# Two-layer conditioned transformer block on one core: three changes in the order of work (ScalarE's last exponentials, the stack's read, the second layer's value projection)

## The chip, the cores and the metric

One of the eight cores of a Trainium2 chip runs the whole kernel. The metric is the device time in microseconds (us) of one execution, a median over executions. The engines are TensorE (PE, with its weight loads as PEld), VectorE (DVE), ScalarE (ACT), GpSimd (POOL) and SyncE (SP), which here issues every DMA.

## The reference, cut to what matters

The input is 16 sequences of 256 tokens by 256 features, a condition of 64 numbers for each sequence, and one mask for all. Two layers follow each other, each added to its input.

```
# layer 0, for each sequence
n1 = g1(cond) * x * rsqrt(mean(x*x) + eps) + b1(cond)
a  = x + softmax(q(n1) k(n1)^T / 4) v(n1) @ Wo.T          # 16 heads of 16, no mask
n2 = g2(cond) * a * rsqrt(mean(a*a) + eps) + b2(cond)
x  = x + a + (silu(n2 @ gate.T) * (n2 @ hid.T)) @ out.T    # hidden 1024
# layer 1
o  = softmax(mask(q(x) k(x)^T / 4)) v(x) @ Wo.T            # the mask hides keys, the same for all queries
x  = x + (o * rsqrt(mean(o*o) + eps) * rms_scale) * (1 + sc(cond)) + shift(cond)
```

## The kernel before, in words

Matmuls of fp32 precision are made from three passes over high and low parts (`mm3`, lines 526 to 528). All 16 sequences stay in SBUF (`X`). The work is a software pipeline over 32 items: item n below 16 is sequence n in layer 0, the others are layer 1. Step s (from -3 to 33) works on several items at once (`stages`, line 79): A, the query and key projection of item s+2; V and B1, the value projection and the first score pass (for the row maxima) of item s+1; B2, the second score pass with the exponentials of item s; C, the division, output projection and mean squares of item s-1; C2 and C3, the gated feed-forward part of layer-0 items s-2 and s-3; R, the output norm of layer 1, item s-2; N, the input norm of item s+3. Each step has eight slots g = 0 to 7; slot g carries heads 2g and 2g+1 of both score passes. Every engine's order is written out by hand in its own `step` function, and engines meet at semaphores only. Steps 3 to 12 and 19 to 28 are loops of two steps.

TensorE's results of A, V, C and the norms go through two PSUM banks in turn, `work0` and `work1`. `bank_uses` (line 105) lists the uses of a step in order; the uses take the two banks alternately, and a use waits (`open_bank`) until the use before it on its bank is freed. From step 19 on the shift rows' and output norm's small uses have a third bank (`acc`). In steps 19 to 29 the list is Q, T1a, T1b, K, T2, Wo, V, ms on banks 0, 1, 0, 1, 0, 1, 0, 1. K is freed by VectorE's `rest` (line 924), T2 by its `ol` (line 910), which the output projection also needs as an operand.

Queries and keys: each projection is split in three bf16 parts (ScalarE L1100 and L1149, VectorE L920 and L924, GpSimd L1239), written to DRAM (`write_parts`, L414), and when both writes have landed read back (`read_stack`, L424) so that the parts of 96 contraction rows stand on 96 partitions. One half (8 heads) is three DMAs of 384, 256 and 128 KB in pieces of 4096 bytes, all on SP's queue. SP's order in a step is: shift rows of half 1, query write, key write, stack read of half 0, shift rows of half 0 (`rows_in(0)`, L470), result store (R), stack read of half 1. TensorE waits for half 0 ahead of the first score pass of slot 0 in the next step and for half 1 at slot 4 (`scores_for_max`, L569 or L584). Ahead of the second score pass (`scores`, L607) of slots 0 and 4 it waits for the shift rows, the negated row maxima that SP copies into the stack.

The mask of the input hides all keys of the first half, which the kernel finds at run time; layer 1's score passes then take the second key half alone (`full` is False).

ScalarE in slot 7 of a step with a layer-0 item in C: it waits for VectorE's product of the residual and the second norm's root (`crm`, L955), applies gain and bias (`affine`, L1087, twice), copies to the high part `xch` (L1134), and then does the two exponentials of slot 7 (`exps`, L1058). GpSimd makes the low part `xcl` (L1322) from `xch`; the first feed-forward matmul of the next step needs it. The second half's probability-value product (`values(st, 1)`, L623) stands at slot 0 of the next step and needs all exponentials.

Slot 3 of a layer-1 step on TensorE: first and second score pass, output projection of item s-1, value projection of item s+1. ScalarE then copies the output projection to `y` (L1162) and the values to `vaug` (L1166); GpSimd squares `y` (L1298) for the mean squares at slot 6 (L710).

Of the kernel before, what the change touches and what calls it, by code (L numbers as in the profile page):

```python
# [46 lines left out]
T = 256  # L47
D = 256
H = 16
# [21 lines left out]
FIRST, LAST = -3, 2 * B + 1  # L71
SPARE = B + 3


# [30 lines left out]
def bank_uses(L):  # L105

    uses = []
    for g in range(SLOTS):
# [8 lines left out]
        if g == 2 and L["C"] is not None:  # L117
            uses.append("T2")
        if g == 3 and L["C"] is not None:
            uses.append("Wo")  # L120
        if g == q_slot(L, 1):
            uses.append("K")
        if g == 1 and L["R"] is not None:
            uses.append("bcR")
        if g == 3 and L["V"] is not None:
            uses.append("V")
# [105 lines left out]
def build(nc, xT, w0, w_ffn, w_out, w1, condT, cond_w, cond_b, rms_scale, mask, maskT, yT):  # L232
    ctx = ExitStack()
    with ctx:
# [114 lines left out]
        q_written, k_written = sem("q_written"), sem("k_written")  # L349
        stack_loaded = [sem(f"stack_loaded{i}") for i in range(2)]  # L350
        s1_full, s1_free = sem("s1_full"), sem("s1_free")
# [33 lines left out]
        def _(sp):  # L385
# [29 lines left out]

            def read_stack(par, half_):

                row = 0
                for parts in (3, 2, 1):
                    k = DH * parts  # L420
                    src = bass.AP(scr[par].tensor, half_ * 6 * DH * 8 * T,
                                  [[8 * T, k], [(6 * DH - k) * 8 * T, 2], [1, 8 * T]])
                    dst = stack[par][row:row + k, :, 8 * half_:8 * half_ + 8, :]
                    sp.dma_start(dst.rearrange("r o h t -> r o (h t)"), src).then_inc(stack_loaded[half_], 16)  # L424
                    row += k
# [13 lines left out]
            def step(st):  # L439
# [50 lines left out]
                if L["A"] is not None:  # L490
                    for half_ in range(2):
                        after(sp, stack_loaded[half_], scratch_read)
                    after(sp, q_low, a_split)
                    write_parts(par, 0, qp, q_written)
                    after(sp, k_low, a_split)
                    write_parts(par, 3 * DH, kp, k_written)
                    after(sp, q_written, a_written)
                    after(sp, k_written, a_written)
                    if L["B2"] is not None:
                        after(sp, s2_full, heads_used[0])  # L500
                    mask_row_in(st, 0)
                    read_stack(par, 0)
                load_swap(6)
                if L["B1"] is not None:
# [3 lines left out]
                if L["A"] is not None:  # L508
                    if L["B2"] is not None:
                        after(sp, s2_full, heads_used[1])  # L510
                    mask_row_in(st, 1)
                    read_stack(par, 1)
                for r in registers:
# [7 lines left out]
        def _(pe):  # L521
# [31 lines left out]
            def scores_for_max(st, g):  # L553
                n, par = st.n(1), 1 - st.par
                if g in (0, 4):
                    after(pe, stack_loaded[g // 4], 48 * (n + 1))
                    if st.s0 in (BRANCH, BRANCH + 1):
                        pe.wait_ge(mask_row_loaded[g // 4], 16 * (st.s0 - BRANCH + 1))
# [184 lines left out]
            def step(st):  # L743
# [14 lines left out]
                for g in range(SLOTS):  # L758
# [24 lines left out]
                    if g == 5 and L["B1"] is not None and st.s0 >= SPARE:  # L783
                        shift_transpose(st, 0)
                    if g == 3 and L["C"] is not None:
                        if st.s0 - 1 == B:
# [6 lines left out]
                    if g == 1 and L["R"] is not None:  # L793
                        broadcast_rstd(st, "bcR", 2)
                    if g == 3 and L["V"] is not None:
                        if st.s0 + 1 == B:
# [235 lines left out]
        def _(act):  # L1032
# [51 lines left out]
            def affine(st, buf, gain, shift, b, done, count):  # L1084
# [5 lines left out]
                after(act, done, count)  # L1090

            def shift_store(st, half_):
                bank, free = opened(st, f"sh{half_}")
# [13 lines left out]
            def step(st):  # L1107
# [5 lines left out]
                for g in range(SLOTS):  # L1113
# [12 lines left out]
                    if g == 6 and st.s0 >= SPARE:  # L1126
                        if L["B1"] is not None:
                            shift_store(st, 0)
                    if g == 7 and L["C"] == 0:
                        n = st.n(-1)  # L1130
# [3 lines left out]
                        a.copy(xch[1 - st.par][:, :, :], crm[:, :, :]).then_inc(c_hi, 1)  # L1134
                    if L["B2"] is not None:
                        exps(st, g)
                        if g == 1:
                            shift_store(st, 1)
                    if g == 5 and st.s0 < SPARE:
# [10 lines left out]
                    if g == 2 and L["R"] is not None:  # L1150
                        n = st.n(-2)
                        b, k = st.bank("bcR")
                        after(act, work_free[b], k + 1)
                        affine(st, crm, C_SCALE, C_SHIFT, n - B, c_affine, 2 * (n + 1))
                    if g == 3 and L["C"] == 1:
                        bank, free = opened(st, "Wo")
# [5 lines left out]
                        a.copy(flat(y[:, :, :]), bank[:, :]).then_inc(free, 1)  # L1162
                    if g == 3 and L["V"] is not None:
                        bank, free = opened(st, "V")
                        after(act, pv_done, 2 * st.n(0))
                        a.copy(vaug[1 - st.par][:, :, :, 0:DH],  # L1166
                               bank[:, :].rearrange("p (t h d) -> p t h d", t=TC, h=H)).then_inc(free, 1)
                    if g == 4 and L["N"] == 1:
# [218 lines left out]
```

## Time and profile before

| | |
|---|---|
| time, median of 3 executions | 999.9 us (996.64, 999.9, 1002.29) |
| the profiled execution: time, span | 992.56 us, 990.5 us |
| busy PE, PEld, DVE, ACT, POOL | 92%, 79%, 58%, 53%, 42% |
| mean granted TensorE clock | 0.963 |
| DMA, share of 16 engines | 40.4% |

The span is that of the trace; the execution's own time has 2.06 us more around it. Matmuls are pipelined and their ends are modelled, so a busy PE row says that TensorE has work and not that it runs at its peak; the waits ahead of single instructions say more. In rows of the timeline the bracket gives the idle time of that engine ahead of the row and what ended it. The clock of 1.00 is 2.4 GHz, 0.50 is 1.2 GHz.

### The profile page before, as it was taken

To read this page: it belongs to the slowest core of one execution; us is meant where nothing else is said; L and a number is where in the kernel's file an instruction comes from. 1 tells how busy PE (TensorE), PEld (TensorE's weight loads), DVE (VectorE), ACT (ScalarE), POOL (GpSimd) and SP (SyncE) were. 2 spreads that over 40 slices of the span, in tenths; PEclk is the share of its full clock that TensorE was granted. 3 is DMA by queue.
4 is the path that set the end of the run, shared out by engine and by line. 5 is a ranking of instruction groups with operands and counts; after the bars stand their busy time and mean duration, and the time that the engine had idled before them with its cause. 6 is when DMAs were issued, how large, how long until landed. Compare 5 with 4: busy or idle time off the path is not lost.

```text
span 990.5 us, 24274 instructions
## 1 busy us (share of the span) xinstructions
PE 910.0 (92%) x8188; PEld 777.7 (79%) x8188; DVE 575.3 (58%) x1136; ACT 529.9 (53%) x1098; POOL 416.2 (42%) x633
## 2 busy tenths in 40 slices
PE   3578899999999999999999999999998999999884
PEld 3456598898988988889888898898887777777653
DVE  3366557556665565555755656645646666666541
ACT  2246446546455464555654654554546566666552
POOL 5233343434443434434443443444444545454422
PEclk9779799999999999999999999999999999999986
DMA  6555422422233223322242233234236767676801
GB/s 201 117 107 125 91 66 61 92 66 44 69 86 59 65 59 71 82 44 65 63 86 64 51 91 86 50 67 91 67 64 143 174 146 171 150 171 150 175 21 34
DMA packets 81724, 91.27 MB, mean 92 GB/s; under 512 B 6432, under 2 KB 68672, under 8 KB 81664
## 3 DMA queue, kind: packets, MB, share of 16 engines
q1 hardware_dynamic: 81664, 90.49, 40.4%
q8 instruction: 35, 0.57, 0.3%
q14 instruction: 25, 0.20, 0.1%
HBM read 60.30 MB, written 29.36 MB: 91 GB/s over the span
## 4 chain that ended last, share of the span: by engine, by line
PE 72%; DMA 8%; DVE 6%; issue 5%; ACT 5%; POOL 2%; SPq 1%; ACTq 0%; POOLq 0%; DVEq 0%
PE work L526 12%; PE work L527 11%; PE work L528 11%; PE pvps L623 8%; PE s2ps L607 6%; PE s1ps L584 5%; DMA stack<-scr 5%; PE work L710 3%; PE work L656 3%; PE acc L526 3%; PE acc L527 2%; PE acc L528 2%; DMA scr<-kp 2%; PE s1ps L569 2%; ACT E L1058 1%
## 5 line engine op out<-in xcount | busy, mean ns | idle before, releaser
L1058 ACT ACTIVATE E<-s2ps 128x512 f32<-128x512 f32 x384 | 214.0, 596 | 179.9 <-PE s2ps L607 113.6
L883 DVE TENSOR_REDUCE nmax<-s1ps 128x2 f32<-128x512 f32 x256 | 164.0, 683 | 32.2 <-PE s1ps L584 32.0
L963 DVE SCALAR_TENSOR_TENSOR th<-th,work 128x256 f32<-128x256 f32 x128 | 54.0, 422 | 174.5 <-ACT th L1076 174.5
L526 PE MATMUL work<-xch,Gh 128*128 128x256 f32 x512 | 154.6, 302 | 0.0
L1336 POOL TENSOR_TENSOR hl<-hf,hh 128x256 fp32r<-128x256 f32 x128 | 94.9, 742 | 132.9 <-PE acc L528 76.7
L527 PE MATMUL work<-xcl,Gh 128*128 128x256 f32 x512 | 146.3, 286 | 0.0
L528 PE MATMUL work<-xch,Gl 128*128 128x256 f32 x512 | 146.2, 286 | 0.0
L607 PE MATMUL s2ps<-stack 100*128 100x256 bf16 x768 | 129.2, 277 | 0.2
L876 DVE TENSOR_REDUCE nmax<-s1ps 128x4 f32<-128x512 f32 x128 | 85.6, 686 | 38.0 <-PE s1ps L569 37.8
L623 PE MATMUL pvps<-E,vaug 128*32 128x256 f32 x1536 | 99.1, 392 | 8.0 <-ACT E L1058 7.0
L526 PEld LDWEIGHTS work<-xch,Gh 128*128 128x128 f32 x512 | 98.8, 193 | 8.1 <-issue 6.6
L527 PEld LDWEIGHTS work<-xcl,Gh 128*128 128x128 f32 x512 | 99.2, 194 | 0.3
L528 PEld LDWEIGHTS work<-xch,Gl 128*128 128x128 f32 x512 | 99.2, 194 | 0.0
L584 PE MATMUL s1ps<-stack 96*128 96x256 bf16 x512 | 83.4, 283 | 11.6 <-DVE nmax L883 5.4
L1239 POOL TENSOR_TENSOR qp<-rest,qp 128x512 bf16<-128x512 f32 x32 | 37.2, 1164 | 134.5 <-ACT qp L1105 118.5
L1076 ACT ACTIVATE th<-work 128x256 f32<-128x256 f32 x128 | 49.2, 384 | 70.2 <-PE work L528 70.2
L526 PE MATMUL work<-xnh,Wh 128*128 128x256 f32 x256 | 78.9, 308 | 3.6 <-DVE on L903 0.9
L1239 POOL TENSOR_TENSOR kp<-rest,kp 128x512 bf16<-128x512 f32 x32 | 37.2, 1164 | 103.4 <-DVE rest L924 48.8
L623 PEld LDWEIGHTS pvps<-E,vaug 128*32 128x32 f32 x1536 | 44.5, 111 | 43.9 <-issue 15.5
L607 PEld LDWEIGHTS s2ps<-stack 100*128 100x128 bf16 x768 | 67.9, 99 | 12.0 <-issue 0.8
L527 PE MATMUL work<-xnl,Wh 128*128 128x256 f32 x256 | 74.1, 289 | 0.0
L528 PE MATMUL work<-xnh,Wl 128*128 128x256 f32 x256 | 73.9, 289 | 0.0
(133 smaller groups left out, 2171.8 us busy)
## 6 DMA issues: line engine op xcount, KB each, us to landing
stack<-scr SPq DMA_DIRECT2D x64, 384.0 KB, 4.6
stack<-scr SPq DMA_DIRECT2D x64, 256.0 KB, 5.3
scr<-qp SPq DMA_DIRECT2D x64, 192.0 KB, 2.3
scr<-kp SPq DMA_DIRECT2D x64, 192.0 KB, 2.3
stack<-scr SPq DMA_DIRECT2D x64, 128.0 KB, 5.6
X<-xT SPq DMA_DIRECT2D x16, 256.0 KB, 4.6
yT<-crm SPq DMA_DIRECT2D x16, 256.0 KB, 2.5
E<-w_ffn SPq DMA_DIRECT2D x2, 1024.0 KB, 6.0
```

Source lines behind the costliest of these rows:

```text
L526: mm(out, lh, rh, start=first, stop=False, skip_group_check=True)
L527: mm(out, lh, rl, start=False, stop=False, skip_group_check=True)
L528: return mm(out, ll, rh, start=False, stop=last, skip_group_check=True)
L584: last = mm(bank[:, T * i:T * (i + 1)], qst[par][0:PARTS, h, P * qh:P * (qh + 1)], kst[par][0:PARTS, h, :], start=st.L["B1"] == 0, stop=Tr ...
L607: last = mm(bank[:, T * i:T * (i + 1)], kst[par][0:ROWS, h, P * kh:P * (kh + 1)], qst[par][0:ROWS, h, :], start=not add_mask, stop=True, s ...
L623: last = mm(pvps[32 * i:32 * (i + 1), T * (j % 2):T * (j % 2 + 1)], v_of[:, kh, h, :], E[:, exp_slot(layer, st.full, h // 2, kh), T * (h % ...
L876: v.tensor_reduce(nmax[:, g // 4, :, 2 * (g % 4):2 * (g % 4) + 2], s1ps[g % 2][:, :].rearrange("p (q h t) -> p q h t", q=2, h=2), AX_X, AL ...
L883: v.tensor_reduce(nmax[:, g // 4, qh, 2 * (g % 4):2 * (g % 4) + 2], s1ps[u % 2][:, :].rearrange("p (h t) -> p h t", h=2), AX_X, ALU.max, n ...
L963: v.scalar_tensor_tensor(th[:, i % 2, :], th[:, i % 2, :], 1.0, bank[:, 0:T], ALU.add, ALU.mult).then_inc(silu_ready, 1)
L1058: a.activation(E[:, exp_slot(st.L["B2"], st.full, g, kh), :], s2ps[g % 2 if short else u % 2][:, :], ACT.Exp, scale=SCORE_SCALE).then_inc( ...
L1239: p.tensor_tensor(parts[:, lo_at, :, :], rest[:, :, :], parts[:, 1, :, :], ALU.subtract).then_inc(low, 1)
L1336: p.tensor_tensor(hl[:, i % 2, :], hf[:, i % 2, :], hh[:, i % 2, :].bitcast(F32), ALU.subtract).then_inc(h_low, 1)
```

## The change

It has three parts. On ScalarE, the exponentials of a slot are put ahead of the layer-0 output norm's gain and bias (this differs in slot 7 alone). On SP, the stack's half 0 is read in two pieces, heads 0 to 3 and heads 4 to 7, each of three DMAs in pieces of 2048 bytes, both behind the same waits; TensorE waits for the first piece at slot 0, for the second at slot 2, and for half 1 at slot 4 as it did. In steps 17 to 30, where C is in layer 1, the value projection precedes the output projection on TensorE, in the list of banks and on ScalarE.

```diff
+HEADS = ((0, 0, 4), (0, 4, 4), (1, 0, 8))
 # bank_uses
+        if g == 3 and L["V"] is not None and L["C"] == 1:
+            uses.append("V")
         if g == 3 and L["C"] is not None:
             uses.append("Wo")
...
-        if g == 3 and L["V"] is not None:
+        if g == 3 and L["V"] is not None and L["C"] != 1:
             uses.append("V")
 # SP
-            def read_stack(par, half_):
+            def read_stack(par, piece):
+                half_, first, heads = HEADS[piece]
                 row = 0
                 for parts in (3, 2, 1):
                     k = DH * parts
-                    src = bass.AP(scr[par].tensor, half_ * 6 * DH * 8 * T,
-                                  [[8 * T, k], [(6 * DH - k) * 8 * T, 2], [1, 8 * T]])
-                    dst = stack[par][row:row + k, :, 8 * half_:8 * half_ + 8, :]
-                    sp.dma_start(...).then_inc(stack_loaded[half_], 16)
+                    src = bass.AP(scr[par].tensor, half_ * 6 * DH * 8 * T + first * T,
+                                  [[8 * T, k], [(6 * DH - k) * 8 * T, 2], [1, heads * T]])
+                    h0 = 8 * half_ + first
+                    dst = stack[par][row:row + k, :, h0:h0 + heads, :]
+                    sp.dma_start(...).then_inc(stack_loaded[piece], 16)
                     row += k
...
                     read_stack(par, 0)
+                    read_stack(par, 1)
                 load_swap(6)
                 if L["B1"] is not None:
                     rows_in(0)
...
-                    read_stack(par, 1)
+                    read_stack(par, 2)
 # TensorE
             def scores_for_max(st, g):
+                if g in (0, 2, 4):
+                    after(pe, stack_loaded[g // 2], 48 * (n + 1))
                 if g in (0, 4):
-                    after(pe, stack_loaded[g // 4], 48 * (n + 1))
...
+                    if g == 3 and L["V"] is not None and L["C"] == 1:
+                        value_projection(st)
                     if g == 3 and L["C"] is not None:
...
                         output_projection(st)
...
-                    if g == 3 and L["V"] is not None:
+                    if g == 3 and L["V"] is not None and L["C"] != 1:
 # ScalarE
+                    if L["B2"] is not None:
+                        exps(st, g)
+                        if g == 1:
+                            shift_store(st, 1)
                     if g == 7 and L["C"] == 0:
                         ...
                         affine(st, crm, C_G2, C_B2, n, c_affine, 2 * (n + 1))
                         a.copy(xch[1 - st.par][:, :, :], crm[:, :, :]).then_inc(c_hi, 1)
-                    if L["B2"] is not None:
-                        exps(st, g)
-                        if g == 1:
-                            shift_store(st, 1)
...
+                    if g == 3 and L["V"] is not None and L["C"] == 1:
+                        value_store(st)      # the copy to vaug
                     if g == 3 and L["C"] == 1:
                         ...
                         a.copy(flat(y[:, :, :]), bank[:, :]).then_inc(free, 1)
```

With the new list, steps 19 to 29 use the banks as Q 0, T1a 1, T1b 0, K 1, T2 0, V 1, Wo 0, ms 1.

## Rows read from the trace of the kernel before

**Rows 1.** The page: busy us, share of the span, instructions.
```profile
PE 910.0 (92%) x8188; PEld 777.7 (79%) x8188; DVE 575.3 (58%) x1136; ACT 529.9 (53%) x1098; POOL 416.2 (42%) x633
```

**Rows 2.** Stretches: us from:to, length, busy (x count) by engine, PEclk, DMA, GB/s.
```profile
436.41:475.94 39.53, 39.07 (x357) 34.92 (x357) 23.90 (x47) 21.88 (x49) 16.64 (x25) 1.00 0.31 67
395.36:436.41 41.05, 40.59 (x357) 36.43 (x357) 23.87 (x47) 21.99 (x49) 16.61 (x25) 0.96 0.30 64
425.30:428.60 3.30, 3.30 (x18) 3.30 (x17) 0.84 (x3) 2.21 (x6) 1.49 (x2) 0.50 0.01 2
850.00:882.90 32.90, 30.55 (x312) 24.77 (x316) 21.93 (x45) 20.92 (x41) 17.03 (x29) 1.00 0.70 161
```

**Rows 3.** Timeline, TensorE, values at slot 0: start, us, what, idle before.
```profile
155.09 0.42 PE L623 MATMUL pvps<-E,vaug 128*32 128x256 f32 x4 [0.28 <-ACT E L1058]
...
273.75 0.63 PE L623 MATMUL pvps<-E,vaug 128*32 128x256 f32 x7 [0.36 <-ACT E L1058]
...
554.92 0.64 PE L623 MATMUL pvps<-E,vaug 128*32 128x256 f32 x8 [0.28 <-ACT E L1058]
...
114.07 1.51 PE L623 MATMUL pvps<-E,vaug 128*32 128x256 f32 x12 [1.03 <-issue]
```

**Rows 4.** Timeline, ScalarE, slot 7 of the step ending at 273.7.
```profile
270.88 1.10 ACT L1087 ACTIVATE crm<-crm,cond 128x256 f32<-128x256 f32 x2 [1.40 <-DVE crm L955]
...
272.54 1.08 ACT L1058 ACTIVATE E<-s2ps 128x512 f32<-128x512 f32 x2
```

**Rows 5.** Timeline, weight loads: last scores of that slot, next feed-forward matmul.
```profile
270.09 0.43 PEld L607 LDWEIGHTS s2ps<-stack 100*128 100x128 bf16 x4
...
276.39 0.19 PEld L526 LDWEIGHTS work<-xch,Gh 128*128 128x128 f32 x1
```

**Rows 6.** Timeline, GpSimd, same place.
```profile
272.71 1.28 POOL L1322 TENSOR_TENSOR xcl<-crm,xch 128x512 fp32r<-128x512 f32 x1 [2.43 <-ACT xch L1134]
```

**Rows 7.** Timeline, TensorE, one layer-1 step.
```profile
839.89 0.40 PE L569 MATMUL s1ps<-stack 97*128 97x128 bf16 x4 [0.29 <-DMA stack<-scr]
840.12 0.38 PE L607 MATMUL s2ps<-stack 100*128 100x256 bf16 x2
...
843.57 0.60 PE L718 MATMUL acc<-dg,ones 128*128 128x256 f32 x2
...
846.40 0.39 PE L526 MATMUL work<-oh,Wh 128*128 128x256 f32 x1 [0.91 <-DVE ol L910]
...
851.67 1.05 PE L710 MATMUL work<-mean,dg 128*128 128x1 f32 x8
```

**Rows 8.** Timeline, VectorE, same step.
```profile
845.07 0.68 DVE L924 TENSOR_TENSOR rest<-work,kp 128x512 f32<-128x512 f32 x1
845.66 0.68 DVE L910 TENSOR_TENSOR ol<-work,oh 128x512 fp32r<-128x512 f32 x1
```

**Rows 9.** Timeline, ScalarE and GpSimd, same step.
```profile
848.91 0.58 ACT L1162 COPY y<-work 128x512 f32<-128x512 f32 x1
...
849.65 1.04 POOL L1298 TENSOR_TENSOR dg<-y 128x512 f32<-128x512 f32 x1
```

**Rows 10.** Timeline, SP, DMA issues of one layer-1 step.
```profile
833.31 1.27 SPq L424 DMA_DIRECT2D stack<-scr  x3
836.06 0.74 SPq L470 DMA_DIRECT2D stack<-rows  x1
```

**Rows 11.** Chain of waits: start, us to landing, what.
```profile
834.15 5.62 DMA stack<-scr
...
83.36 4.67 DMA stack<-rows
```

**Rows 12.** The page, DMA issues: KB each, median us to landing.
```profile
scr<-kp SPq DMA_DIRECT2D x64, 192.0 KB, 2.3
```

**Rows 13.** Waits, whole span: us in total, times, longest.
```profile
PE s1ps L569 <- DMA stack<-scr: 4.4, 7, 1.4
```

**Rows 14.** Timeline, TensorE, first score pass of the run.
```profile
44.62 1.04 PE L584 MATMUL s1ps<-stack 96*128 96x256 bf16 x4 [4.62 <-DMA stack<-scr]
```

More of the change, by code:

```diff
@@ L349, in build @@
         q_written, k_written = sem("q_written"), sem("k_written")
-        stack_loaded = [sem(f"stack_loaded{i}") for i in range(2)]
+        stack_loaded = [sem(f"stack_loaded{i}") for i in range(3)]
         s1_full, s1_free = sem("s1_full"), sem("s1_free")
@@ L420, in read_stack @@
                     k = DH * parts
-                    src = bass.AP(scr[par].tensor, half_ * 6 * DH * 8 * T,
-                                  [[8 * T, k], [(6 * DH - k) * 8 * T, 2], [1, 8 * T]])
-                    dst = stack[par][row:row + k, :, 8 * half_:8 * half_ + 8, :]
-                    sp.dma_start(dst.rearrange("r o h t -> r o (h t)"), src).then_inc(stack_loaded[half_], 16)
+                    src = bass.AP(scr[par].tensor, half_ * 6 * DH * 8 * T + first * T,
+                                  [[8 * T, k], [(6 * DH - k) * 8 * T, 2], [1, heads * T]])
+                    h0 = 8 * half_ + first
+                    dst = stack[par][row:row + k, :, h0:h0 + heads, :]
+                    sp.dma_start(dst.rearrange("r o h t -> r o (h t)"), src).then_inc(stack_loaded[piece], 16)
                     row += k
@@ L490, in step @@
                 if L["A"] is not None:
-                    for half_ in range(2):
-                        after(sp, stack_loaded[half_], scratch_read)
+                    for piece in range(3):
+                        after(sp, stack_loaded[piece], scratch_read)
                     after(sp, q_low, a_split)
@@ L1090, in affine, with value_store @@
                 after(act, done, count)
+            def value_store(st):
+                bank, free = opened(st, "V")
+                after(act, pv_done, 2 * st.n(0))
+                a.copy(vaug[1 - st.par][:, :, :, 0:DH],
+                       bank[:, :].rearrange("p (t h d) -> p t h d", t=TC, h=H)).then_inc(free, 1)
             def shift_store(st, half_):
@@ L1162, in step @@
                         a.copy(flat(y[:, :, :]), bank[:, :]).then_inc(free, 1)
[L1163 to L1167, printed above, removed]
+                    if g == 3 and L["V"] is not None and L["C"] != 1:
+                        value_store(st)
                     if g == 4 and L["N"] == 1:
```

## The prediction

> **What bounds the kernel now.** I read the page first, then the stretches, then the waits ahead of single TensorE instructions. TensorE is busy for 92% of the span [rows 1]. A layer-0 step takes 39.53 us with 39.07 busy, so there only TensorE's own gaps can be won [rows 2]. A layer-1 pair of steps takes 32.90 us, 16.45 a step, with 30.55 busy and DMA at 0.70 [rows 2]: there TensorE and a loop through DRAM are nearly level. Three waits are what the change can touch: the values at slot 0 wait for ScalarE's exponentials [rows 3], the output projection waits 0.91 us for `ol`, and the first score pass waits for the stack [rows 7, 13].
>
> **Part 1, exponentials first.** In slot 7 ScalarE runs the two gains from 270.88, then `xch`, and the exponentials only from 272.54 to 273.62 [rows 4]; TensorE starts the values at 273.75 after 0.36 us of idling for them [rows 3]. Their scores were loaded from 270.09 to 270.52 [rows 5], with the last product some 0.3 us later, so the exponentials could run from about 270.8 to 271.9, long before TensorE wants them. The whole wait goes. It stands ahead of eleven boundaries from 155.09 to 554.92, nine at about 0.36 us and the two ends at 0.28 [rows 3]. As the rows' ends are modelled and a restart costs a little more than the idle figure, I count 0.40 each, 4.4 us; the bounds are 0 and 0.5 each (5.5). The boundary at 114.07, at half clock, waits 1.03 us, and there the exponentials would come some 1.1 us sooner; I take 0.9 (0 to 1.0). What is late in return is `xch`, by the 1.08 us of the exponentials, and with it `xcl`: 272.71 + 1.28 = 273.99 becomes 275.1 [rows 4, 6]. The next step's first feed-forward matmul, loaded at 276.39 [rows 5] and now 0.4 earlier, still finds it 0.9 us old. GpSimd's queue behind `xcl` moves back by the same 1.1 us, and nothing in it is waited for sooner than that matmul. ScalarE's total is the same. Part 1: -5.3 us.
>
> **Part 2, the value projection first.** The first read says 0.91 us won in each of eleven steps (19 to 29). It isn't so: the value projection takes the bank that K held, which VectorE's `rest` frees at 845.07 + 0.68 = 845.75, while `ol` ends at 845.66 + 0.68 = 846.34 [rows 8]. TensorE can start 0.59 us sooner and no more. The output projection behind it then finds `ol` done. ScalarE now copies the values (0.58 us, taken from the like copy) before `y`, so `y` ends at 848.91 + 0.58 + 0.58 = 850.07, its square (now 849.65 to 850.69) at about 851.2, and the mean squares, at 851.67 now [rows 7, 9], would be wanted at 851.08: a new wait of 0.1 us. So TensorE's own path of a step shrinks by about 0.5 us. Whether that counts depends on the loop in part 3. In steps 17 and 18 the banks leave the start of slot 3 where it was, and step 30 has no K: nothing there.
>
> **Part 3, the stack in two pieces.** The key write lands, three reads go out from 833.31, the last lands at 834.15 + 5.62 = 839.77 [rows 10, 11], the first score pass starts at 839.89 and the second at 840.12; K's projection is done when the next instruction starts at 843.57 [rows 7], and the loop starts again. A 192 KB write lands in 2.3 us [rows 12], which I take as a DMA's fixed part. From the first issue to the last landing are 6.46 us, 4.2 of them for 768 KB; a first piece of half the bytes lands 2.1 us sooner, at 837.7 (bounds: not sooner at all, or half of 6.46, 3.2 us). The three added issues cost SP 1.27 us [rows 10], from 834.58 to 835.9, and the shift rows' issue was at 836.06: it just fits. The second piece is wanted at slot 2, near 844, and lands near 840: hidden.
>
> But the first score pass was not alone. Right behind it the second pass needs the shift rows, issued at 836.06 behind all six stack DMAs on one queue [rows 10]. They landed before 840.12, and no sooner than 2.3 us after issue, 838.4. The row at 83.36 shows such rows taking 4.67 us with a read ahead of them [rows 11]; I put them with the end of the read, about 839.6. The change moves neither the read's last byte nor these rows. TensorE would do the first score pass early and then stand at the second until 839.6 or a little later, where it now starts at 840.12. So the step loses 0.5 us at best, and the 0.5 us of part 2 falls into the same wait. Over the steps 20 to 30 the trace puts 4.4 us of idling to the stack, in seven waits [rows 13]; I take 4.4 less 1.4 for 2048-byte pieces and more issues ahead of the shift rows: -3.0 us. Bounds: +4 (rows 0.4 us later in eleven steps) and -10.9 (4.4 and 0.59 times eleven, if the rows don't bind).
>
> At the start of the run TensorE stands 4.62 us for the first stack [rows 14], and no shift rows are needed in that step; the 2.1 us are won there, but a half-clock stretch follows, so I take 1.5 (0 to 3.2). In layer 0's later steps no first score pass waits for a stack, so an earlier one wins nothing.
>
> The Trainium skill (DMA: Bandwidth & Descriptors, the anatomy of one DMA) fits a GpSimd-issued DMA as 2.0 us plus bytes at 436 GB/s. By it, 384 KB less would land only 0.9 us sooner, and the run's start would win 0.9 at most; the sum would be 9.2 instead of 9.8. This trace's 4.2 us for 768 KB is 187 KB/us, less than half of that rate, so I go by the trace.
>
> **The sum.** 5.3 + 3.0 + 1.5 = 9.8 us, the profiled execution's 992.56 would become 982.8 (span 990.5 to 980.7). The median shown is 999.9, 7.3 above that execution. Three layer-0 steps in a row took 41.05 instead of 39.53 us, each with 3.3 us at a clock of 0.50 (1.2 GHz) around the mean squares [rows 2]; if the median's excess is the same thing, it has nearly five more. The steps keep the same work but get another length, and a run of equal steps would break up; I allow two fewer, 3 us. Predicted: 999.9 - 9.8 - 3 = 987.1, say 987 us.
>
> **Rivals.**
> (a) The shift rows don't bind and TensorE's path decides: layer 1 gives 10.9 - 1.1 = 9.8 instead of 3.0, and with fewer half-clock stretches 978 to 981 us. For it: no wait of the second score pass for rows is in the layer-1 rows. Against: the first pass hid it. Chance 0.25.
> (b) The read in two pieces and the new order bring nothing, and part 1 brings its 4 to 5 us alone: 995 us. For it: the DMA share of 0.70 and the shift rows' place in the queue. Chance 0.2. If even part 1's wait is replaced (`xcl` more than 0.9 us later than I think), the change does nothing: 999 to 1000, included here.
> (c) Slower: a read is paid by the piece and not by the byte. Half 0 has twice the pieces, so its 4.2 us become 8.4, and the shift rows behind it land 4.2 us later; each of eleven steps waits 4.2 - 0.5 longer, +41, less 6.8 from parts 1 and the start: near 1034. It makes the kernel slower from about 1.1 us a step on ((6.8 + 5)/11). Against: a 192 KB write in pieces of 512 bytes, eight times as many per byte, lands in 2.3 us [rows 12]. Chance 0.05.
> The forecast itself (984 to 993) has 0.5.
>
> **How the numbers follow.** 0.5% of 999.9 is 5 us, about what a measurement can tell; faster is below 994.9. The forecast's case and (a) are faster nearly whole (0.5 and 0.25, less 0.04), (b) in a quarter: 0.76. Within 0.5%: 0.18. Slower: (c) and a bad draw of half-clock stretches, 0.06. The range takes (a) in to 975 and (b) to 997.
>
> **What would show it.** Right: values at slot 0 with no idle for ScalarE in the eleven boundaries and `xch` a microsecond later; layer-0 steps of 39.1 us; in layer 1 the value projection starting as `rest` ends; first score passes starting early, and the second ones idling behind them for the shift rows; a step of 16.0 to 16.3 us. Wrong: second score passes right behind the first ones and steps of 15.6 (then (a)); shift rows landing more than 4 us after issue (then (b) or (c)); feed-forward matmuls waiting for `xcl`; layer-0 steps that stay at 39.5.

## The result, and the profile after

The changed kernel takes 975.87 us (median of four runs, 973.7 to 977.97) against 1000.53 us for the kernel before (four runs, 996.64 to 1002.29). The ratio is 0.9758 [0.9722, 0.9795]: 24.7 us less. The forecast was 987 us, a gain of 13. The profiled execution took 973.7 us with a span of 971.6 us, at a mean granted clock of 0.971; before it was 992.56, 990.5 and 0.963. Line numbers are higher after the change: `rest` is L933, `ol` L919, the score passes L576 or L591 and L614, `mm3` L532 to L534, the exponentials L1067.

The page, busy time, as in [rows 1]; then the shares of the chain that ended last. TensorE's share of the chain was 72% before and DMA's 8%.

```profile
PE 905.2 (93%) x8188; PEld 774.5 (80%) x8188; DVE 574.7 (59%) x1136; ACT 526.0 (54%) x1098; POOL 413.2 (43%) x633
```

```profile
PE 85%; DVE 5%; ACT 3%; issue 3%; DMA 2%; POOL 1%; SPq 1%; POOLq 0%; DVEq 0%; ACTq 0%
```

The stretches, as [rows 2]: a layer-0 step with a half-clock stretch, one without, the half-clock stretch itself, and two layer-1 steps.

```profile
345.85:386.46 40.61, 40.51 (x357) 36.32 (x357) 23.98 (x47) 21.89 (x50) 16.54 (x24) 0.96 0.29 65
425.55:464.64 39.09, 38.99 (x357) 34.88 (x357) 23.89 (x47) 21.78 (x50) 16.57 (x24) 1.00 0.30 68
376.10:379.50 3.40, 3.40 (x18) 3.31 (x17) 1.24 (x3) 2.13 (x6) 1.63 (x2) 0.50 0.01 4
836.06:868.15 32.09, 30.78 (x310) 24.72 (x309) 21.92 (x45) 20.43 (x42) 16.62 (x28) 1.00 0.66 165
```

Layer-0 steps went from 39.53 to 39.09 us, and from 41.05 to 40.61 where a half-clock stretch falls in. Two layer-1 steps went from 32.90 to 32.09 us.

The boundaries of [rows 3] on TensorE: the values at slot 0 follow with no idle time in the bracket.

```profile
266.13 1.93 PE L630 MATMUL pvps<-E,vaug 128*32 128x256 f32 x32
...
542.84 0.42 PE L630 MATMUL pvps<-E,vaug 128*32 128x256 f32 x4
```

ScalarE there, as [rows 4], then GpSimd, as [rows 6]. The exponentials now run before the two gains. Against the values at 266.13 the gains start 1.73 us earlier, where they started 2.87 earlier before, so against the values `xch` is 1.1 us later. `xcl` ends at 267.51 and the next step's first feed-forward matmul is at 268.80: 1.3 us of room, where the prediction had 0.9. It had delayed the gains by the whole 1.08 us of the exponentials on the step's own clock; as the values come 0.43 us sooner too, they are only 0.7 later there.

```profile
263.43 1.09 ACT L1067 ACTIVATE E<-s2ps 128x512 f32<-128x512 f32 x2 [1.14 <-PE s2ps L614]
264.40 1.09 ACT L1096 ACTIVATE crm<-crm,cond 128x256 f32<-128x256 f32 x2
265.52 0.62 ACT L1153 CAST xch<-crm 128x512 fp32r<-128x512 f32 x1
```

```profile
266.22 1.29 POOL L1336 TENSOR_TENSOR xcl<-crm,xch 128x512 fp32r<-128x512 f32 x1 [3.12 <-ACT xch L1153]
```

One layer-1 step on TensorE, as [rows 7]: the third line is the transposes of item s-1's output in slot 1, the last is now the value projection, which waits for `rest`. The two passes of slot 0, shown ahead of them, have no idle in front.

```profile
842.29 0.40 PE L576 MATMUL s1ps<-stack 97*128 97x128 bf16 x4
842.52 0.38 PE L614 MATMUL s2ps<-stack 100*128 100x256 bf16 x2
843.06 0.66 PE L663 MATMUL work<-ident,oT 128*128 128x128 f32 x4 [0.15 <-ACT oT L1077]
...
848.59 0.35 PE L532 MATMUL work<-Wh,xnh 128*128 128x256 f32 x1 [0.40 <-DVE rest L933]
```

VectorE there, as [rows 8]: `rest` ends at 848.44, and the value projection starts at 848.59, 0.45 us before `ol` ends.

```profile
847.76 0.68 DVE L933 TENSOR_TENSOR rest<-work,kp 128x512 f32<-128x512 f32 x1
848.36 0.68 DVE L919 TENSOR_TENSOR ol<-work,oh 128x512 fp32r<-128x512 f32 x1
```

SP's issues in such a step, as [rows 10]:

```profile
836.48 2.68 SPq L429 DMA_DIRECT2D stack<-scr  x6
839.25 0.74 SPq L475 DMA_DIRECT2D stack<-rows  x1
```

The first score pass of the run, as [rows 14]: 42.22 instead of 44.62 us, 2.15 of idling instead of 4.62.

```profile
42.22 1.03 PE L591 MATMUL s1ps<-stack 96*128 96x256 bf16 x4 [2.15 <-DMA stack<-scr]
```

Where 18.9 us of span went, read from the starts of the values in both timelines: 2.1 by the first one (77.60 to 75.47). 4.2 between there and 155.09 (now 148.78). A stretch at half clock, 107.7 to 118.0 us before, is absent after, so these 4.2 have two causes. The kernel with the exponentials undone (`e_noexps` below) has no such stretch either, and from the values at 82.24 to those at 149.44 it takes 67.20 us, against 65.46 after and 69.65 before: 1.7 are the exponentials' and 2.5 the clock's. 5.8 over the next ten boundaries, 0.43 each and 1.5 for one half-clock stretch fewer. Minus 1.3 for a half-clock stretch at 734.5 us that is new. 5.1 over the layer-1 steps up to 932. 4.6 in step 30, of which 0.8 are its path (14.41 against 15.25 us in kernels without a half-clock stretch there) and 3.7 the half-clock stretch of before at 937.2. Minus 1.3 near the end, another stretch at half clock, and minus 0.2 behind the last values. Together the edits make about 14 and the clock about 5. The boundary behind the missing stretch, as the last of [rows 3], in the changed kernel and then in `e_noexps`:

```profile
109.64 1.24 PE L630 MATMUL pvps<-E,vaug 128*32 128x256 f32 x17 [0.57 <-issue]
```

```profile
110.28 1.07 PE L630 MATMUL pvps<-E,vaug 128*32 128x256 f32 x16 [2.27 <-issue]
```

The rows of the two stretches before, and of the first one's place after (columns as in [rows 2], clock third from last):

```profile
107.70:118.00 10.30, 8.56 (x51) 4.43 (x50) 4.19 (x8) 6.10 (x13) 3.68 (x7) 0.50 0.49 93
937.20:947.40 10.20, 8.25 (x52) 5.72 (x41) 3.23 (x7) 2.97 (x6) 0.66 (x3) 0.50 0.49 106
```

```profile
107.70:118.00 10.30, 8.82 (x86) 6.43 (x84) 6.81 (x15) 7.07 (x14) 3.35 (x6) 1.00 0.51 102
```

### The profile page after: what moved, and what is told of

The parts are those of the page before. It is cut to its first block, busy times and chain, and to the rows that moved or that the text cites. A ratio compares the mean times of both kernels' runs of the same rounds, so it can differ in the third digit from the quotient of the medians.

```text
span 971.6 us, 24412 instructions
## 1 busy us (share of the span) xinstructions
PE 905.2 (93%) x8188; PEld 774.5 (80%) x8188; DVE 574.7 (59%) x1136; ACT 526.0 (54%) x1098; POOL 413.2 (43%) x633
## 4 chain that ended last, share of the span: by engine, by line
PE 85%; DVE 5%; ACT 3%; issue 3%; DMA 2%; POOL 1%; SPq 1%; POOLq 0%; DVEq 0%; ACTq 0%
PE work L532 14%; PE work L533 12%; PE work L534 12%; PE pvps L630 9%; PE s2ps L614 7%; PE s1ps L591 6%; PE work L717 4%; PE work L663 3%; PE acc L532 3%; PE acc L533 3%; PE acc L534 3%; PE s1ps L576 2%; PE work L725 1%; PE work L677 1%; DVE rest L933 1%
## 5 line engine op out<-in xcount | busy, mean ns | idle before, releaser
L1067 ACT ACTIVATE E<-s2ps 128x512 f32<-128x512 f32 x384 | 214.9, 598 | 192.9 <-PE s2ps L614 126.8
L532 PE MATMUL work<-xch,Gh 128*128 128x256 f32 x512 | 154.0, 301 | 0.1
L534 PE MATMUL work<-xch,Gl 128*128 128x256 f32 x512 | 145.6, 284 | 0.0
L614 PE MATMUL s2ps<-stack 100*128 100x256 bf16 x768 | 127.6, 275 | 1.0 <-DMA stack<-rows 0.8
L532 PEld LDWEIGHTS work<-xch,Gh 128*128 128x128 f32 x512 | 98.2, 192 | 8.5 <-issue 6.9
L534 PEld LDWEIGHTS work<-xch,Gl 128*128 128x128 f32 x512 | 98.6, 193 | 0.0
L591 PE MATMUL s1ps<-stack 96*128 96x256 bf16 x512 | 83.2, 282 | 8.4 <-DVE nmax L892 5.4
L532 PE MATMUL work<-xnh,Wh 128*128 128x256 f32 x256 | 79.3, 310 | 3.6 <-DVE on L912 0.9
L614 PEld LDWEIGHTS s2ps<-stack 100*128 100x128 bf16 x768 | 67.1, 98 | 13.1 <-issue 1.7
L534 PE MATMUL work<-xnh,Wl 128*128 128x256 f32 x256 | 74.0, 289 | 0.0
```

The costliest lines, as they stand in the source:

```text
L532: mm(out, lh, rh, start=first, stop=False, skip_group_check=True)
L534: return mm(out, ll, rh, start=False, stop=last, skip_group_check=True)
L591: last = mm(bank[:, T * i:T * (i + 1)], qst[par][0:PARTS, h, P * qh:P * (qh + 1)], kst[par][0:PARTS, h, :], start=st.L["B1"] == 0, stop=Tr ...
L614: last = mm(bank[:, T * i:T * (i + 1)], kst[par][0:ROWS, h, P * kh:P * (kh + 1)], qst[par][0:ROWS, h, :], start=not add_mask, stop=True, s ...
L1067: a.activation(E[:, exp_slot(st.L["B2"], st.full, g, kh), :], s2ps[g % 2 if short else u % 2][:, :], ACT.Exp, scale=SCORE_SCALE).then_inc( ...
```

## Experiments

All were timed beside runs of the kernel before on the same chip. A ratio is to that kernel. "Layer-1 step" is the mean of eight steps, from the values of one step near 771 to 790 us to the same eight steps on: 16.59 us before and 16.11 after, each with a few tenths of disturbance in single steps; the undisturbed steps are 16.41 and 16.47 in turn before, and 16.01 and 16.08 after.

**One part at a time.** The first kernel is the changed one with the other two parts undone:

```diff
 # e_exps: changed kernel, value projection and stack read as before
-                    if g == 3 and L["V"] is not None and L["C"] == 1:
-                        value_projection(st)
...
-HEADS = ((0, 0, 4), (0, 4, 4), (1, 0, 8))
+HEADS = ((0, 0, 8), (1, 0, 8))
```

> Only the exponentials of slot 7 go ahead of the layer-0 output norm's gains; the stack's read and the order of the two projections are those of before. Theory (each part pays where its own wait stands): the eleven boundaries from 155 to 555 us lose 0.43 us each, 4.7 us, the boundary at 114 about 1, so 5 to 6 us, ratio 0.994 to 0.995; layer-1 steps stay at 16.46 us. Rival (most of the 24.7 us comes from half-clock stretches that go away once these waits are gone): 10 us or more, ratio 0.990 or lower, with the stretches at 107 to 118 and at 937 to 947 us missing in the trace.

Measured: 987.85 us, ratio 0.9912 [0.9882, 0.9943]. Layer-0 steps 39.10 us, layer-1 steps 16.59 as before. The order of the exponentials is worth its 0.43 us at each boundary, and there is no half-clock stretch at 107 us either, while the one of 10.2 us near 937 is one of 3.4 at 945. The theory's path of 5 to 6 us is there (4.3 at ten boundaries, 1.7 ahead of them), but its ratio of 0.994 to 0.995 is touched by the interval's edge only. The 0.9912 lies between it and the rival's 0.990: beyond the path, fewer and shorter half-clock stretches brought the rest.

```diff
 # e_value: kernel before, with in layer 1
+                    if g == 3 and L["V"] is not None and L["C"] == 1:
+                        value_projection(st)
                     if g == 3 and L["C"] is not None:
```

> Only the value projection goes ahead of the output projection in layer 1. Theory (in layer 1 the loop through DRAM binds, so TensorE's shorter path falls into the wait for the stack): a layer-1 step stays within 0.1 us of 16.46, ratio 0.998 to 1.001, with the first score pass idling 0.5 us longer for the stack. Rival (TensorE's own path binds): 0.5 us a step in eleven steps, ratio 0.994.

Measured: 995.11 us, ratio 0.998 [0.9957, 1.0004], layer-1 step 16.46. That is what the theory said, but partly by chance: one of the eight steps took 18.04 us, with 2.36 of waiting for the stack. The other seven are 16.05 to 16.46, 16.23 in the mean, 0.2 us less than the undisturbed steps before.

```diff
 # e_split: kernel before, with
+HEADS = ((0, 0, 4), (0, 4, 4), (1, 0, 8))
```

> Only the stack's half 0 is read in two pieces. Theory (the six DMAs of 2048-byte pieces land as a whole about 0.8 us sooner than the three of 4096, and the shift rows behind them too; TensorE's path with its 0.98 us stand ahead of the output projection then binds): layer-1 steps of 16.2 to 16.3 us instead of 16.46, 2.1 us won at the start, 4 to 5 us in all without clock effects, ratio 0.994 to 0.996. Rival (the early first piece is what pays, in full): steps of 15.9 to 16.0.

Measured: 992.18 us, ratio 0.9937 [0.9906, 0.9969]. The start is 2.1 us shorter; layer-1 step 16.44, undisturbed ones 16.41 and 16.47 as before. Both the theory's steps (16.2 to 16.3) and the rival's (15.9 to 16.0) are missed, though the ratio is the theory's: what was won lies at the start and in the clock and the disturbed steps.

```diff
 # e_late: e_split, with
-                if g in (0, 2, 4):
-                    after(pe, stack_loaded[g // 2], 48 * (n + 1))
+                if g == 0:
+                    after(pe, stack_loaded[0], 48 * (n + 1))
+                    after(pe, stack_loaded[1], 48 * (n + 1))
```

> As the kernel with only the read in two pieces, but TensorE waits for both pieces at slot 0. Theory (faster landing of the whole half): layer-1 steps as in the kernel with the early wait, within 0.1 us, the half complete 5.5 to 5.7 us after the key write instead of 6.3 to 6.8; the start of the run wins about 1 us less. Rival (the early wait is what pays): steps of 16.4 us or more, time as before, ratio 0.998 to 1.002.

Measured: 993.32 us, ratio 0.9962 [0.9936, 0.9987]. Layer-1 steps as in e_split apart from one disturbed step, start 0.6 us shorter than before instead of 2.1. As layer 1 had won nothing in e_split, this run tells only of the start. The three parts alone sum to 0.9% + 0.2% + 0.6% = 1.7%; together they bring 2.4%. With intervals of 0.2 to 0.4 points each way and half-clock stretches that differ, these sums say little by themselves; the steps say more. What is missing sits for the most part in layer 1, and TensorE's waits over the eight steps say why (us in total, times, longest). Before:

```profile
PE work L526 <- DVE ol L910: 7.2, 8, 0.9
PE s1ps L569 <- DMA stack<-scr: 3.2, 5, 1.4
```

The value projection first, alone:

```profile
PE s1ps L575 <- DMA stack<-scr: 6.5, 8, 2.4
PE work L531 <- DVE rest L932: 3.2, 8, 0.4
```

The stack in two pieces, alone:

```profile
PE work L530 <- DVE ol L915: 7.2, 8, 0.9
PE work L661 <- ACT oT L1073: 1.1, 7, 0.2
```

Both, in the changed kernel:

```profile
PE work L532 <- DVE rest L933: 3.2, 8, 0.4
PE work L663 <- ACT oT L1077: 0.9, 6, 0.2
PE s2ps L614 <- DMA stack<-rows: 0.8, 1, 0.8
```

Alone, the new order turns 7.2 us of waiting for `ol` into 3.2 for `rest` and gives 3.3 of the 4.0 to the stack, which is now waited for in every step. Alone, the read in pieces ends the wait for the stack, but the transposes of slot 1 then wait for ScalarE's copy `oT`, and `ol` costs what it did. Only together both are gone, and what is left is `rest`, 0.4 us a step.

**The changed kernel without one part.** The exponentials undone:

```diff
 # e_noexps: changed kernel, with exps(st, g) behind the affine of slot 7 again
```

> The changed kernel with the exponentials of slot 7 put back behind the output norm's scale; the early value projection and the read in two pieces stay. Theory J (these two belong together, and the exponentials have their own part): layer-1 steps stay at 16.05 us; layer-0 boundaries come back to a step of 39.53 us, 0.43 us each over eleven of them and some 2 us at the one at 110 us, so the span is 971.6 + 4.7 + 2.2 = 978.5 us if the half-clock stretches stay as in the changed kernel (ratio about 0.983). Theory S (the 39.53 us step brings the half-clock stretches back, eight of 1.5 us in a row as in the kernels with one of the other parts alone, against two): 9 us more, span 987 to 988, ratio 0.989 to 0.992. Rival: the layer-1 gain needs the exponentials too: steps of 16.4 us, 5 us more on either.

Measured: 985.76 us, ratio 0.989 [0.9856, 0.9924]. Layer-1 steps are 16.01 to 16.10 but for one with a wait for shift rows, so layer 1 doesn't need the exponentials. Its layer-0 steps are 39.51 us and six of them in a row have a half-clock stretch, against two in the changed kernel; the rows (columns as in [rows 2]) show one step without and one with:

```profile
268.05:307.56 39.51, 39.05 (x356) 34.90 (x357) 23.88 (x47) 21.86 (x49) 16.61 (x25) 1.00 0.30 67
371.50:412.50 41.00, 40.55 (x358) 36.41 (x357) 23.92 (x48) 21.98 (x48) 16.61 (x25) 0.96 0.30 64
```

So theory S is right in direction, with six stretches for its eight; its ratio (from 0.989) is just reached, but the profiled span of 980.5 us is nearer theory J's 978.5. The part is worth 1.3% here and 0.9% alone, of which 6.0 us, 0.6%, are TensorE's waits (0.43 at each of ten boundaries and 1.7 ahead of them), the rest the clock.

```diff
 # e_nov: changed kernel, with the value projection behind the output projection again
```

> The changed kernel without the early value projection: exponentials first and the read in two pieces alone. Theory J (the two pieces shorten a layer-1 step only together with the early value projection, since without it the output projection waits for `ol` whatever the stack does): layer-1 steps 16.4 us, some 5 us slower than the changed kernel, ratio to the kernel before 0.980 to 0.985. Rival (the value projection is not needed for it): steps 16.05 to 16.1, ratio 0.975 to 0.978.

Measured: 981.95 us, ratio 0.9875 [0.9815, 0.9935], layer-1 step 16.43 with the 7.2 us of waiting for `ol`. The step confirms theory J. The ratio's interval is wide, but it lies wholly above the rival's 0.975 to 0.978.

**Why the shift rows came sooner.** The forecast's loop needed the shift rows to land when they did before. In the changed kernel six DMAs carry the bytes of three. Is it their number or their packets? The next kernel has the same six issues on SP, the same bytes and the same waits as e_late, but splits queries from keys and leaves the packets at 4096 bytes:

```diff
 # e_six: kernel before, half 0 read by
+                    for o in range(2):       # 0: queries, 1: keys
+                        src = bass.AP(scr[par].tensor, o * (6 * DH - k) * 8 * T, [[8 * T, k], [1, 8 * T]])
+                        dst = stack[par][row:row + k, o, 0:8, :]
```

> The kernel before with one edit: half 0 of a stack is read by six DMAs instead of three, one for the queries and one for the keys of each block of rows, each packet still 4096 bytes; the first pass waits for all six. It tells why the split half lands sooner as a whole than the unsplit one. Theory N (the number of transfers in flight): the half and the shift rows behind it land some 0.8 us sooner after the key write, as with the half in two pieces that are both waited for, the start is some 0.6 us shorter, ratio to the kernel before 0.994 to 0.998, layer-1 steps 16.4. Theory P (the 2048-byte packets): the half lands as late as in the kernel before, three more issues, ratio 0.999 to 1.003, start unmoved.

Measured: 994.66 us, ratio 0.9978 [0.9953, 1.0003], layer-1 steps 16.41 to 16.63 but for one. The first values come 1.1 us later than before, but the first score pass of the run only 0.2 (44.85 against 44.62): the first half-clock stretch is 17.1 us long here instead of 13.7, so theory P's unmoved start holds as far as the read goes. Theory P's time and theory N's don't exclude each other by the ratio, but the landings do. Issues of the page, KB each and median us to landing, e_six first, then the changed kernel (the row of 128 KB is left out, as it mixes the second reads of half 0 with the third of half 1):

```profile
stack<-scr SPq DMA_DIRECT2D x64, 192.0 KB, 3.6
...
stack<-scr SPq DMA_DIRECT2D x64, 64.0 KB, 4.1
```

```profile
stack<-scr SPq DMA_DIRECT2D x64, 192.0 KB, 3.1
...
stack<-scr SPq DMA_DIRECT2D x64, 64.0 KB, 3.3
```

Same sizes, same number, and the ones with packets of 2048 bytes land 0.5 and 0.8 us sooner. The two kernels also differ in what a DMA holds, four heads of queries and keys against eight of either; that was not tried apart, and neither were three DMAs of 2048-byte packets. In one step of the timeline: the three reads of before,

```profile
stack<-scr SPq DMA_DIRECT2D x1, 384.0 KB, 4.6
stack<-scr SPq DMA_DIRECT2D x1, 256.0 KB, 5.3
stack<-scr SPq DMA_DIRECT2D x1, 128.0 KB, 5.6
```

against the second piece's three after:

```profile
stack<-scr SPq DMA_DIRECT2D x1, 192.0 KB, 3.4
stack<-scr SPq DMA_DIRECT2D x1, 128.0 KB, 3.3
stack<-scr SPq DMA_DIRECT2D x1, 64.0 KB, 3.3
```

Before, the last read lands 6.46 us after the first issue (833.31 to 839.77 [rows 10, 11]). After, the sixth issue leaves at about 838.7 (836.48 and five sixths of 2.68) and lands 3.3 us on, at 842.0, 5.5 us after the first. It is 0.9 us sooner although its last issue is 1.4 us later. Over the layer-1 steps between 766 and 905 us, by the landing times of their traces, half 0 is complete 6.2 to 6.8 us after its first issue before (median 6.3), 6.2 to 6.8 in e_six (6.4) and 5.4 to 6.1 in the changed kernel (5.6).

```diff
 # e_four: changed kernel, with
-HEADS = ((0, 0, 4), (0, 4, 4), (1, 0, 8))
+HEADS = ((0, 0, 2), (0, 2, 2), (0, 4, 4), (1, 0, 8))
```

> The changed kernel with the first piece of half 0 split again into heads 0 and 1 and heads 2 and 3, waited for at slots 0 and 1. Theory W (layer 1 waits no longer for the stack; only the start does): the start shortens by 0 to 0.8 us, the rest is unmoved, ratio to the kernel before 0.974 to 0.977. Rival P (1024-byte packets cost more per byte, and the rows behind them land later): layer-1 steps of 16.3 us or more and 4 us slower, ratio above 0.979.

Measured: 980.09 us, ratio 0.9834 [0.9797, 0.987], layer-1 step 16.28 with one of 17.19; the other seven are 16.15 in the mean, 0.1 above the changed kernel's. Rival P's time, and TensorE's waits over eight steps name the place:

```profile
PE s2ps L615 <- DMA stack<-rows: 4.1, 8, 1.4
PE work L533 <- DVE rest L934: 3.2, 8, 0.4
```

SP's issues in one of these steps, then the second pass of slot 0 in it:

```profile
837.75 4.11 SPq L429 DMA_DIRECT2D stack<-scr  x9
```

```profile
844.44 0.39 PE L615 MATMUL s2ps<-stack 100*128 100x256 bf16 x2 [0.48 <-DMA stack<-rows]
```

Nine issues take 4.1 us of SP, and the shift rows behind them come too late in every step: this is what the forecast had feared of six. Packet size and number of issues both change here, but the trace points to the issues: the last read leaves 1.4 us later than in the changed kernel (3.65 us after the first issue against 2.23) and takes no longer to land (about 3.0 us against 3.3), so the half is complete only after 6.4 to 6.7 us. The second pass starts within 0.2 us of that moment in every step, so the shift rows do land with the end of the read, as the forecast assumed. Of three, six and nine DMAs, six were best.

```diff
 # e_after_late: changed kernel, both pieces waited for at slot 0 (as e_late)
```

> The changed kernel, its half 0 still read in two pieces, but both waited for ahead of slot 0's first pass. In the changed kernel the second piece landed at 842.0 us and that pass began at 842.29. Theory P (what layer 1 gains from the read is that smaller packets bring the whole half and the shift rows behind it sooner, not that the first pass needs half of it): layer-1 steps 16.0 to 16.15 us as in the changed kernel, and only the start is longer, by 1 to 2 us; ratio to the kernel before 0.976 to 0.981. Rival F (the first pass must start on the first piece): steps of 16.3 us or more, 4 us and the start on top, ratio 0.981 to 0.986.

Measured: 978.51 us, ratio 0.9806 [0.977, 0.9842]. The start is 2.1 us longer; seven of the eight layer-1 steps are 16.01 to 16.09, and the eighth has a wait of 2.0 us for the stack and a half-clock stretch. The ratio lies where the two forecasts meet; the steps decide. So layer 1 doesn't need the first piece early; it needs the whole half sooner, and the early first wait pays at the start.

**Two tries for more.** Half 1 in two pieces as well:

```diff
 # e_half1: changed kernel, with
+HEADS = ((0, 0, 4), (0, 4, 4), (1, 0, 4), (1, 4, 4))
```

> The changed kernel with half 1 of a stack also read in two pieces of four heads, waited for at slots 4 and 6. Theory W (nothing waits for half 1 in the changed kernel, what counts is what its first passes wait for): the same time, 974 to 978 us, ratio to the kernel before 0.974 to 0.978. Rival L (the half and the mask and shift rows behind it land sooner and layer 1 or the start has a wait on them): 2 to 4 us less, ratio 0.971 to 0.974. Rival I (three more issues on SyncE push the next step's rows back): 2 us or more slower, ratio above 0.979.

Measured: 973.4 us, ratio 0.9774 [0.9737, 0.9812]. The intervals of this and of the changed kernel cover each other: the same, theory W. Its layer-1 steps are the changed kernel's.

Then the wait for `rest`, filled with the two passes of slot 4:

```diff
 # e_move: changed kernel; e_best: with half 1 in two pieces too
                         scores(st, g)
+                    if g == 4 and L["V"] is not None and L["C"] == 1:
+                        value_projection(st)
+                    if g == wo_slot(L) and g == 4:      # layer 1
+                        output_projection(st)
```

> The changed kernel with layer 1's value and output projections moved from the end of slot 3 to slot 4, behind its two score passes (on ScalarE and in the order of banks too). In the changed kernel the value projection starts 0.40 to 0.47 us late, waiting for VectorE's `rest`; the two passes of slot 4 take about 0.45 us and need nothing of it. Theory A (that wait is time on the path): it goes, layer-1 steps 15.6 to 15.8 us, some fifteen of them, 4 to 6 us less than the changed kernel, ratio to the kernel before 0.970 to 0.973. Rival B (half 1 of the stack, which landed at 847.8 us where the pass would now start at 848.0, takes its place): steps 15.8 to 16.0, ratio 0.973 to 0.976. Rival C (the output norm comes later and ScalarE is late for the exponentials): steps above 16.05, ratio above 0.977.

> The same move, with half 1 of a stack also read in two pieces of four heads, waited for at slots 4 and 6: the first of them lands some 2.3 us sooner after the key write than the whole half. Theory A: steps 15.6 to 15.7 us with or without it, the same time as with the move alone. Rival B (half 1 is what binds after the move): 0.1 to 0.3 us a step less than with the move alone, 2 to 4 us in all, ratio 0.968 to 0.972. Rival C: as with the move alone, above 0.977.

Measured: 1003.52 us, ratio 1.0092 [1.0063, 1.0121], and 1003.76 us, 1.0097 [1.0067, 1.0126]. Rival C has the sign, but none of the three the cause. TensorE around slot 4 of e_move:

```profile
842.04 0.39 PE L581 MATMUL s1ps<-stack 97*128 97x128 bf16 x4
842.26 0.38 PE L619 MATMUL s2ps<-stack 100*128 100x256 bf16 x2
844.75 0.40 PE L581 MATMUL s1ps<-stack 97*128 97x128 bf16 x4 [2.10 <-DVE nmax L895]
```

and VectorE:

```profile
841.61 0.69 DVE L939 TENSOR_TENSOR kp<-work,kp 128x512 bf16<-128x512 f32 x1 [1.31 <-ACT kp L1174]
842.21 0.68 DVE L943 TENSOR_TENSOR rest<-work,kp 128x512 f32<-128x512 f32 x1
842.81 0.68 DVE L929 TENSOR_TENSOR ol<-work,oh 128x512 fp32r<-128x512 f32 x1
843.41 0.68 DVE L974 TENSOR_TENSOR crm<-y,acc 128x512 f32<-128x512 f32 x1
844.00 1.28 DVE L895 TENSOR_REDUCE nmax<-s1ps 128x4 f32<-128x512 f32 x2
```

The first score passes of slots 2 and 3 fill both banks of row maxima. VectorE empties them only behind `kp`, `rest`, `ol` and `crm`, which is to say from 844.0 us, and the pass of slot 4 stands 2.10 us for it, in each of eight steps. In the changed kernel the two projections are what TensorE does during this backlog. The steps grow by 1.7 us. It stays unexplained why every second or third of them has a half-clock stretch as well (19.3 us instead of 17.8).

No version that was run beats the changed kernel beyond its interval.

## Why the prediction was right or wrong

- **The time** was 11 us too high. It is inside the range only because the range took rival (a) in down to 975; the forecast's own mechanism had 984 to 993. The edits made 14 for 9.8, the clock 5 for 3 in the profiled pair, and the medians differ by 5.8 us more than the spans do. That last part fits a median execution before with more half-clock stretches than the profiled one, as assumed, but no trace of such an execution was taken: it stays open.
- **Exponentials first**, forecast 4.4 us at eleven boundaries and 0.9 at 114: measured 0.43 us at each of the ten behind 155 and 0.35 there, 4.6 in all, and 1.4 at 114, by the kernels without the half-clock stretch; the bound there was 1.0, read from a wait of 1.03 us at half clock that is 2.27 at full clock in `e_noexps`. Right in mechanism and in step length (39.1).
- **Value projection first**, forecast to start as `rest` ends, 0.59 us sooner: right (0.45 us ahead of `ol`'s end). That it brings nothing while the loop binds: right for it alone in the main, 0.998 and 0.2 us in undisturbed steps.
- **The step that failed** is "The change moves neither the read's last byte nor these rows." The rows do land with the read's end (e_four), but that end moved: the last byte came 0.9 us sooner after the first issue, by smaller packets. TensorE starts the second pass 6.04 to 6.07 us after the first issue, the half is complete after 5.4 to 6.1, and the shift rows just don't bind: one wait in eight steps (0.8 us), none of the steady idling that was forecast behind the first pass. The -3.0 for layer 1 became -5.1, and -0.8 in step 30.
- **Rival (a)** had the right mechanism (TensorE's path decides; second passes right behind the first) and the wrong size. It added 4.4 us of stack waits and 0.59 eleven times, for steps of 15.6; measured 16.05. The stack's waits were not to be had in full: e_split ends them and has undisturbed steps no shorter than before (16.41 and 16.47), with 1.1 us of waiting for `oT` over eight steps in place of 3.2 for the stack. Where the rest of them goes is not shown.
- **The start**, forecast 1.5: measured 2.1, the first pass 2.4 us earlier. The 2.1 us of a piece of half the bytes hold: waiting for both pieces costs the first pass 1.9 us (44.01 in e_late, 42.07 in e_split) and 2.1 (44.28 in e_after_late, 42.22). The rest is the whole half landing sooner, 0.6 us in e_late. The Trainium skill's fit for a DMA that GpSimd issues (DMA: Bandwidth & Descriptors, the anatomy of one DMA), by which the prediction estimated 0.9, is too small for these reads.
- **Rival (b)**, that parts 2 and 3 bring nothing, is refuted: part 1 alone is 0.9912, all three 0.9758.
- **Rival (c)**, a price by the piece, is refuted: twice the pieces landed sooner. What nine DMAs lose they lose in SP's issues.
- **The clock**: two fewer half-clock stretches were allowed, and the count went from six to five, not the same ones; the dearest of before (10.2 us long each) are absent or shorter. Which stretches go was not forecast, so the clock's part is luck as much as sense. e_noexps ties the count in layer 0 to the step's length, but loosely (last section).

## What to carry to other kernels

When two waits of one loop run in parallel, price the edits together: either alone can give most or all of its gain to the other wait. For a read whose landing a loop waits for, try smaller packets, and stop before the issues delay what stands behind them in the queue. Before filling a wait of TensorE with other work, look at what VectorE is behind with at that moment.

## What the hardware showed that was not expected

- A half of 768 KB lands 5.5 us after its first issue in six DMAs of 2048-byte packets, and 6.46 in three of 4096; six DMAs of 4096-byte packets needed 6.4 (median of eight steps), with 3.6 us for a read of 192 KB and 4.1 for one of 64, against 3.1 and 3.3.
- The same kernel shape falls into half-clock stretches of 3.4 us, 1.5 us lost each, in eight layer-0 steps in succession in the profiled executions of e_value, e_split, e_late and e_six, and in six of e_noexps, whose steps are 39.5 us. With steps of 39.1 us it was two in the changed kernel, e_four, e_nov and e_move, three in e_exps and e_half1, four in e_after_late and e_best. But the kernel before, with 39.5, had three. One profile of each kernel doesn't settle how much of this is the step and how much the draw.
